# Expert mix shared by ScalarE, VectorE and GpSimd, with plain fp32 matmuls there and in the single-head attention

## The reference

```python
x = x + tanh(g_xattn[0]) * L0_xattn(_layernorm(x), ctx, ...)   # 16 heads of 8
x = x + tanh(g_ffn[0])   * L0_ffn(_layernorm(x), ...)          # 8 experts, 2 per token
x = x + tanh(g_xattn[1]) * L1_xattn(_layernorm(x), ctx, ...)   # 16 heads of 64
x = x + tanh(g_ffn[1])   * L1_ffn(_layernorm(x), ...)          # the expert mix
x = x + tanh(g_xattn[2]) * L2_xattn(_layernorm(x), ctx, ...)   # one head of 128
x = x + tanh(g_ffn[2])   * L2_ffn(_layernorm(x), ...)          # 8 experts, 1 per token
x = x + tanh(g_xattn[3]) * L3_xattn(_layernorm(x), ctx, ...)   # 16 heads of 8
x = x + tanh(g_ffn[3])   * L3_ffn(_layernorm(x), ...)          # ternary weights
```

```python
gate = softmax(x @ gate_w + gate_b)
weights = gate * (gate >= 0.1)
weights = weights / where(sum(weights) == 0, 1, sum(weights))
for e in range(8):
    out = out + weights[:, e:e+1] * (x @ expert_w[e] + expert_b[e])
```

## Time and profile before

| | |
|---|---|
| median of 3 runs | 997.49 us (996.33 to 1000.16) |
| the profiled execution's own time | 996.21 us |
| its span in the profile | 994.4 us, 1.8 us less |
| mean granted TensorE clock | 0.847 |
| PE busy over the span | 767.9 us (77%) |
| DVE | 519.3 us (52%) |
| ACT | 378.3 us (38%) |
| POOL | 278.8 us (28%) |

### The profile page before, as it was taken

One profiled execution on the slowest core, in us unless ns is written; L12 is line 12 of the kernel. 1 busy time (PEld: TensorE's weight loads), 2 busy tenths in 40 slices (PEclk: granted clock), 3 DMA queues, 4 the chain that ended last, 5 costly groups with the idle time before them and its releaser, 6 DMA issues.

```text
span 994.4 us, 18119 instructions
## 1 busy us (share of the span) xinstructions
PE 767.9 (77%) x6805; PEld 652.2 (66%) x6805; DVE 519.3 (52%) x1610; ACT 378.3 (38%) x886; POOL 278.8 (28%) x229
## 2 busy tenths in 40 slices
PE   4789872878959898989997556994486975988874
PEld 3567750777858787979786334774374964767764
DVE  5467461352234776666664878424242333778562
ACT  5455530333424654646461001210132554555450
POOL 4344316514332450212020000000305334344031
PEclk9999795798979999999998877555596986999996
DMA  7533625525733000000001000000432634321001
GB/s 182 131 89 104 195 74 172 136 73 162 208 102 102 19 23 1 2 1 2 1 1 64 0 1 0 1 1 28 147 97 85 181 105 118 104 64 34 1 12 32
DMA packets 60546, 70.95 MB, mean 71 GB/s; under 512 B 7036, under 2 KB 40717, under 8 KB 60461
## 3 DMA queue, kind: packets, MB, share of 16 engines
q1 hardware_dynamic: 57389, 63.48, 22.6%
q0 software_dynamic: 3072, 6.30, 2.1%
HBM read 48.86 MB, written 20.91 MB: 70 GB/s over the span
## 4 chain that ended last, share of the span: by engine, by line
PE 53%; DVE 19%; issue 8%; DMA 7%; ACT 6%; POOL 6%; SPq 0%; POOLq 0%; DVEq 0%; ACTq 0%
PE banks L1346 6%; PE banks L1362 5%; PE banks L1027 4%; PE banks L1438 4%; POOL xs L648 4%; DMA xs<-xn,slot 3%; PE banks L1028 3%; PE banks L1029 3%; DVE x L2221 3%; PE banks L1447 3%; PE banks L1069 3%; PE banks L1458 3%; PE banks L1155 3%; PE banks L1178 2%; PE banks L1167 2%
## 5 line engine op out<-in xcount | busy, mean ns | idle before, releaser
L898 ACT ACTIVATE hT<-banks,wup 128x128 f32<-128x128 f32 x304 | 85.6, 371 | 155.4 <-PE banks L1346 139.2
L1346 PE MATMUL banks<-xTs,wup 128*128 128x128 f32 x608 | 95.2, 309 | 21.2 <-issue 12.9
L1346 PEld LDWEIGHTS banks<-xTs,wup 128*128 128x128 f32 x608 | 88.1, 223 | 25.0 <-issue 24.9
L573 POOL TENSOR_TENSOR kbd<-k,const 96x1248 fp32r<-96x1248 f32 x32 | 72.3, 2266 | 70.4 <-PE banks L1155 68.2
L815 ACT ACTIVATE pT<-banks 77x512 f32<-77x512 f32 x128 | 69.0, 589 | 57.8 <-PE banks L1155 57.7
L1362 PE MATMUL banks<-wd,hT 128*128 x608 | 87.7, 292 | 3.8 <-ACT hT L898 3.8
L556 POOL TENSOR_TENSOR rstd<-vv,const 128x4 f32<-128x4 f32 x24 | 24.3, 1014 | 223.0 <-DVE vv L1662 223.0
L1362 PEld LDWEIGHTS banks<-wd,hT 128*128 128x128 f32 x608 | 81.1, 208 | 4.3 <-issue 4.2
L648 POOL DMA_INDIRECT xs<-xn,slot x48 | 46.5, 969 | 121.8 <-DVE slot L1960 89.8
L2072 DVE COPY ysb<-banks 128x128 f32<-128x128 f32 x76 | 22.0, 289 | 107.9 <-PE banks L1362 93.1
L611 POOL TENSOR_TENSOR sh<-sh,rd 128x616 f32<-128x616 f32 x32 | 38.9, 1216 | 129.4 <-DVE rd L1715 128.8
(11 more groups left out here) (323 smaller groups left out, 1787.3 us busy)
## 6 DMA issues: line engine op xcount, KB each, us to landing
wup<-in_up SPq DMA_DIRECT2D x76, 258.0 KB
q<-queries SPq DMA_DIRECT2D x24, 256.0 KB, 4.3
queries<-qc SPq DMA_DIRECT2D x8, 512.0 KB, 2.7
wd<-in_down SPq DMA_DIRECT2D x8, 512.0 KB, 5.1
ys<-ysb SPq DMA_DIRECT2D x16, 256.0 KB
k<-keys SPq DMA_DIRECT2D x24, 156.0 KB, 3.6
xs<-zt SPq DMA_DIRECT2D x2, 1472.0 KB, 11.5
keys<-kc SPq DMA_DIRECT2D x8, 312.0 KB, 3.4
```

Source lines behind the costliest of these rows:

```text
L573: pool.tensor_tensor(kbd[b % NB8][0:96, :, :, :].bitcast(F32R), kb, m, ALU.mult).then_inc(h8.kbd, 1)
L898: ins = act.activation(hT[T % 3][:, c, :], ps[:, T % 2, c * P:c * P + P], func, bias=wup[T % NW][:, HID + c:HID + c + 1])
L1346: ins = pe.matmul(ps[:, T % 2, c * P:c * P + P], w_[:, c * P:c * P + P], xTs[T % 3][:, :], start=True, stop=True)
```

## The change

In the mix, the products of experts 0 to 3 (i = 0) are made by ScalarE into buffers `mtmp`, those of experts 4 to 7 by VectorE onto `x` as before. GpSimd adds up ScalarE's products and the bias rows and adds the sum to `x` (`mixed_sum`). The units alternate between the two halves (`mixed_unit`). Units and gate logits are single fp32 matmuls on unrounded tokens `xT`, in two buffers; fronts in `PLAIN` (those of both stages) have no remainder. The gate of group g + 1 is computed during group g, that of group 0 and the first two units during the last group of `heads64`; eight small operations follow the exponential instead of eleven. ScalarE normalises the tokens of four fronts that VectorE did. In `head128`, q and both score products are single fp32 matmuls; k and v stay split. The front moves ahead of the second scores, and VectorE adds a group's output one group later. The split of `head128`'s weights moves ahead of the mix. GpSimd no longer splits the expert weights.

```diff
-        ON_ACT = (*range(0, NG), *range(6 * NG, 7 * NG + 1))
+        ON_ACT = (*range(0, NG), *range(3 * NG + 1, 4 * NG + 1), *range(6 * NG, 7 * NG + 1))
+        PLAIN = (*range(3 * NG, 5 * NG),)
...
+            def mixed_sum(g):
+                m = mtmp[g % 2]
+                pool.wait_ge(mx.act, 4 * (g + 1))
+                pool.tensor_tensor(m[:, :, 0:2, :], m[:, :, 0:2, :], m[:, :, 2:4, :], ALU.add).then_inc(su.plink, 1)
+                pool.wait_ge(su.plink, NG + 3 * g)
+                pool.tensor_tensor(m[:, :, 0, :], m[:, :, 0, :], m[:, :, 1, :], ALU.add).then_inc(su.plink, 1)
+                pool.wait_ge(su.plink, NG + 3 * g + 1)
+                pool.wait_ge(mx.xb, g + 1)
+                pool.tensor_tensor(m[:, :, 0, :], m[:, :, 0, :], m[:, :, 4, :], ALU.add).then_inc(su.plink, 1)
+                pool.wait_ge(su.plink, NG + 3 * g + 2)
+                pool.wait_ge(mx.half, 4 * (g + 1))
+                xt = x[:, GB * g:GB * g + GB, :]
+                pool.tensor_tensor(xt, xt, m[:, :, 0, :], ALU.add).then_inc(mx.x, 1)
...
             def mixed():
+                def products(g, t):
+                    if t == 0:
+                        act.wait_ge(mx.c, g + 1)
+                        if g >= 2:
+                            act.wait_ge(mx.x, g - 1)
+                    act.wait_ge(mx.o, 8 * g + 2 * t + 1)
+                    for e in range(4):
+                        ins = copy(mtmp[g % 2][:, t, e, :], ps[:, (8 * g + 2 * t) % 6, e * P:e * P + P],
+                                   scale=cw8[:, GB * (g % 2) + t, e:e + 1])
+                    ins.then_inc(mx.act, 1)
+                for g in range(NG):
+                    n = g + 3 * NG + 1
+                    scaled(next_group(g), n)
+                    products(g, 0)
+                    act.wait_ge(mx.ct_mm, g + 1)
+                    copy(cT[:, 0, :], ps[0:GB * E, 6, 0:P]).then_inc(mx.ct, 1)
+                    products(g, 1)
+                    front(n)
+                    products(g, 2)
+                    act.wait_ge(mx.b_mm, g + 1)
+                    copy(mtmp[g % 2][:, :, 4, :], ps[:, 6, :].rearrange("p (t d) -> p t d", t=GB)).then_inc(mx.xb, 1)
+                    if g < NG - 1:
+                        gate_exp(g + 1)
+                    products(g, 3)
...
+            def mixed_unit(g, v):
+                U, t, i = 8 * g + v, v // 2, v % 2
+                if U >= 6:
+                    pe.wait_ge((mx.act, mx.half)[i], (U - 6) // 2 + 1)
+                pe.matmul(ps[:, U % 6, :], xT[(g + 3 * NG) % 2][:, t * P:t * P + P], l1raw[:, 3, 512 * i:512 * i + 512],
+                          start=True, stop=True).then_inc(mx.o, 1)
             def mixed():
+                for g in range(NG):
+                    for v in range(2 * GB):
+                        if g or v >= 2:
+                            mixed_unit(g, v)
+                        if v == 1:
+                            pe.wait_ge(mx.c, g + 1)
+                            if g:
+                                pe.wait_ge(mx.xb, g)
+                            pe.transpose(ps[0:GB * E, 6, 0:P], ...
+                        if v == 3:
+                            if g:
+                                pe.wait_ge(mx.d, g + 1)
+                            front(g + 3 * NG + 1)
+                            pe.wait_ge(mx.ct, g + 1)
+                            pe.matmul(ps[:, 6, :], cT[:, 0, :], b2m[1]...).then_inc(mx.b_mm, 1)
+                        if v == 5 and g < NG - 1:
+                            mixed_logits(g + 1)
...
-                            ins = split3(ps[:, 3, b * SP:b * SP + SP], tokens([z[:, :] for z in q_], b),
-                                         tuple(z[:, b, :] for z in k_))
+                            ins = pe.matmul(ps[:, 3, b * SP:b * SP + SP], q2[i][:, b * P:b * P + P], k2[i][:, b, :],
+                                            start=True, stop=True)
-                        split3(ps[:, 0, :], tuple(w_[:, 0, :] for w_ in w2), xs).then_inc(h1.qmm, 1)
+                        pe.matmul(ps[:, 0, :], b_raw[:, 0:P], xT[g % 2], start=True, stop=True).then_inc(h1.qmm, 1)
...
+                def during():
+                    mixed_weights(0)
+                    front_a(1, 3 * NG + 1)
+                attend(h64, NG - 1, add, None, during)
...
             def mixed():
+                wait_done(dve, "h64", 1)
+                front_b(1, 3 * NG + 1)
+                dve.wait_ge(mx.c, 1)
+                for g in range(NG):
+                    n = g + 3 * NG + 2
+                    weighted(g, 0)
+                    front_a((g + 2) % NG, n)
+                    weighted(g, 2)
+                    if g < NG - 1:
+                        mixed_gate(g + 1)
+                        front_b((g + 2) % NG, n)
+                        mixed_weights(g + 1)
+                        dve.wait_ge(mx.c, g + 2)
```

More of the change, by code:

```diff
@@ L213, in build @@
         wregion = [top[0], wend]
+        mtmp = [place(f"mtmp{i}", [P, GB, 5, D], F32, wregion) for i in range(2)]
+        wregion = [top[0], wend]
         wf = place("wf", [P, HID], F32R, wregion)
@@ L307, in build, with split_upto @@
         back_in = (mo.gat0, mo.gat1)
-        ON_ACT = (*range(0, NG), *range(6 * NG, 7 * NG + 1))
+        ON_ACT = (*range(0, NG), *range(3 * NG + 1, 4 * NG + 1), *range(6 * NG, 7 * NG + 1))
+        PLAIN = (*range(3 * NG, 5 * NG),)
+        xT = (xT_even[:, :], xT_odd[:, :])
+        def split_upto(n):
+            return sum(m not in DROPPED and m not in PLAIN for m in range(n + 1))
         def shifts(n):
@@ L694, in _ @@
             ins.then_inc(su.scratch, 1)
-            for g in range(0, NG):
-                rsqrt_front(g + 4 * NG + 1)
+            for g in range(NG):
+                rsqrt_front(g + 3 * NG + 2)
+                mixed_sum(g)
+            for g in range(0, NG - 1):
+                rsqrt_front(g + 4 * NG + 2)
             spread(2)
@@ L1466, in heads64, with first_units, mixed_logits @@
                     front(g + 2 * NG + 2)
-                attend(h64, NG - 1, scores, own_values, values, project)
+                mixed_logits(0)
+                def first_units(between):
+                    pe.wait_ge(h64.sub, 4 * B)
+                    mixed_unit(0, 0)
+                    mixed_unit(0, 1)
+                    between()
+                attend(h64, NG - 1, scores, own_values, values, project, first_units)
+            def mixed_logits(g):
+                pe.wait_ge(fr.lo, upto(g + 3 * NG))
+                pe.wait_ge(ld.r, 16 * 9)
+                for t in range(GB):
+                    ins = pe.matmul(ps[:, 7, t * 16:t * 16 + E], xT[(g + 3 * NG) % 2][:, t * P:t * P + P], rraw[:, 0:E],
+                                    start=True, stop=True)
+                ins.then_inc(mx.r, 1)
@@ L1532, in head128 @@
                             o_ = ps[0:SK, 5, b * P:b * P + P]
-                            split3(o_, tuple(z[:, b, 0:SK] for z in k_), tokens([z[:, :] for z in q_], b), stop=False)
+                            pe.matmul(o_, k2[i][:, b, 0:SK], q2[i][:, b * P:b * P + P], start=True, stop=False)
                             ins = pe.matmul(o_, const[0:GB, C_SELB + b * SK:C_SELB + b * SK + SK], nT2[:, :],
@@ L2271, in head128 @@
[L2271 to L2283 removed]
+                        dve.tensor_copy(nT2[:, :], ps[0:GB, 3, 384:384 + P]).then_inc(h1.nT, 1)
```

256 lines of the change are left out of this document (109 added, 147 removed).

## The result

The changed kernel takes 965.54 us (median of 4 runs, 963.98 to 969.16) against 996.91 us (4 runs, 995.85 to 1000.16): ratio 0.9685, 95% interval 0.965 to 0.9721. The forecast was 964 us in a range of 944 to 986. The total was hit, but in part by luck: the mix gained 6.9 us less than forecast, the attention and the stages behind it 8.4 us more, and these misses nearly cancel.

What follows compares the result with a forecast made beforehand. It took the mix as bound by VectorE's serial products and gate, on which TensorE waits, and the attention by TensorE at half clock; 22.4 + 10 = 32.4 us off 996.21 gave 963.8, stated as 964, range 944 to 986.

Steps and rivals of the forecast that it cites:

- start of the mix: Last attention block before the mix: early weights, statistics, two units and logits make it 2.3 us longer.
- weights to end of unit 7, all groups, with last products: Mix: TensorE's stretch after the weights, 8.0 us a group at full clock; group 0 10.0, last products 2.1.
- end of unit 7 to the next weights, 3 x: Mix: landing, products, gate and small operations take 5.0 us between groups, with TensorE idle for 3.2.
- mix in sum: Whole expert mix: 59.4 us against 81.8, 22.4 us less.
- single-head attention: Stage after the mix: 10 us less, bounds 2 and 20.
- 20.2 us a group: Mix: upper bound of a group, six units at 1.71 and the rest doubled, plus 5.0; about 4.5 us less.
- so it hides behind the next group: Mix: GpSimd's sums, 7.5 us a group, are wanted only later and stay hidden, even at twice the cost.
- The rival about GpSimd: Mix: sums over 15 us a group hold back buffers two groups on, about 12 us lost, 976 us; chance 0.06.
- Which of the two depends on the clock at which the stage is entered: Attention: the clock at entry decides between half clock, gaining 2 us, and full clock, gaining 20.
- that is no gain: Attention at half clock: savings and losses of the fp32 products and new order cancel; only the first group gives 2 us.
- 9.7 us for a group at full clock: Attention: a group's period at full clock is 9.7 us, against 14.4 at half clock before.
- Half of 20: Attention: half of the 20 us full-clock gain was taken, 10 less.

Runs made afterwards that it cites:

- e1: Changed kernel without GpSimd's sums in the mix, one add of 8 columns a group instead: 957.0 us, ratio 0.9577.
- e2: Changed kernel with GpSimd's sums started only when the next weights are ready, the last after the next front's normalisation: 957.76 us, ratio 0.9614.
- e8: Changed kernel with GpSimd's first sum of each group cut into eight of 128x128: 965.58 us, ratio 0.9666.
- e3: Changed kernel with the next group's gate and weights placed ahead of VectorE's second pair of tiles: 954.3 us, ratio 0.9525.
- e6: Changed kernel with the gate ahead of VectorE's second pair of tiles and GpSimd's sums held back as well: 952.21 us, ratio 0.9535.
- e4: Changed kernel with four unread fp32 matmuls in each of TensorE's three waits for the weights: 968.49 us, ratio 0.9675.
- e5: Kernel before with only the single-head attention's part of the change (products, order, late addition): 984.53 us, ratio 0.9869.
- e7: Kernel before with only the attention's q and score products as single fp32 matmuls, order unchanged: 987.85 us, ratio 0.9912.

## Why the total was right and three of its terms were not

Ahead of the mix, code that the change does not touch ran 6.9 us longer in the first profiled execution than before and 1.2 in the second, so the spans differ by 27.0 and 32.9 us. The parts from the mix on, measured in the first, add up to 33.9 us less.

| term | predicted us | measured |
|---|---|---|
| start of the mix | +2.3 | +2.2 |
| weights to end of unit 7, all groups, with last products | 42.1 | 40.6 |
| end of unit 7 to the next weights, 3 x | 3 x 5.0 = 15.0 | 3 x 7.8 = 23.4 |
| mix in sum | -22.4 | -15.5 |
| single-head attention | -10 | -14.0 |
| stages behind | 0 | -4.4 |
| total, medians | -32.4 | -31.4 |

(42.1 is the prediction's 10.0 + 3 x 15.0 + 2.1 less the 15.0. Measured are 10.9, 9.6, 9.4 and 10.65. Mix in sum: 2.2 + 64.1 = 66.3 from the same point as in the earlier trace rows, 81.8 there.) Two of the prediction's sums do not come out as written: the parts of the way from unit 7 to the weights make 5.1 us, not 5.0, and 20.2 us a group would be 6.8 us less than before, not 4.5. The first would move the forecast by 0.4 us, the second moves only a bound.

**The failed step is GpSimd's "so it hides behind the next group".** The sums' length was right, and no one waited for their result. But they run beside the gate, and two operations of VectorE stand until they end. Removing the sums (e1), moving them (e2) and cutting them (e8) each take that wait away (2.9, 2.9 and 3.2 us are left of 5.9), so this is shown. The gate's 5.0 us were sound: without the collision it is 7.8 - 3.04 = 4.76, and TensorE's idle 2.9 against 3.2 predicted. The rival about GpSimd looked for the wrong victim: the buffers two groups on, at twice the price, where the victim was the next small operation of VectorE, at the normal price. The Trainium skill has the rule in "GPSIMD Engine Reference", Key points: GpSimd shares its SBUF interfaces with VectorE, and contention arises with VectorE instructions that have two SBUF inputs or run in a 2-port mode. The trace agrees (L2277 has two such inputs, 2.33 us for 0.16). The prediction did not weigh it. It could have: the trace of the kernel before shows such a collision, ahead of the first expert stage (timeline, before). An operation of VectorE on 128x8 elements with two inputs in SBUF lasts 2.23 us and ends 0.03 us behind GpSimd's; its neighbour of the same size takes 0.15.

```profile
98.33 2.27 POOL L573 TENSOR_TENSOR kbd<-k,const 96x1248 fp32r<-96x1248 f32 x1
98.40 2.23 DVE L2026 SCALAR_TENSOR_TENSOR mb<-mv,rstd 128x8 f32<-128x8 f32 x1 [0.79 <-POOL rstd L578]
...
100.55 0.15 DVE L2027 TENSOR_TENSOR rs<-mv,rstd 128x8 f32<-128x8 f32 x1
```

**The gate one group ahead.** That VectorE's order keeps the gate behind unit 7 was read rightly. What that order costs is read from four kernels: with the sums where the change has them 18.1 us of mix (64.0 against e3's 45.9), with the sums moved 9.8 (e2's 53.2 against e6's 43.4). The collision in turn costs 10.8 us of mix with this order (64.0 against 53.2) and 2.5 with the gate first (45.9 against 43.4).

**The clock in the mix.** It fell in each group, but behind idles of 5.9 us where 3.2 were forecast: windows of the changed kernel around the gate of group 1.

```profile
549.60:556.50 6.90, 4.20 (x14) 1.94 (x13) 3.92 (x17) 1.90 (x7) 0.56 (x1) 0.99 0.00 0
556.50:563.30 6.80, 3.58 (x5) 1.44 (x6) 3.45 (x4) 3.28 (x12) 5.57 (x4) 0.50 0.00 1
563.30:573.50 10.20, 7.91 (x27) 3.75 (x25) 7.53 (x37) 3.71 (x12) 1.17 (x2) 1.00 0.00 1
```

And two stretches of e2, behind its first and its third gate, each of 2.9 us idle:

```profile
548.80:552.30 3.50, 3.31 (x5) 1.43 (x6) 0.49 (x2) 3.18 (x12) 3.14 (x2) 0.51 0.01 2
577.15:579.15 2.00, 2.00 (x7) 1.00 (x8) 0.33 (x1) 2.00 (x9) 1.91 (x1) 1.00 0.00 0
```

The changed kernel's burst starts at 0.50 at 559.72 and is at full clock from 563.3. It cost 9.5 us a group for the predicted 8.0, where 2.0 of penalty were allowed. That each burst begins at the low clock after idle time is also the rule quoted in the prediction from the Trainium skill, "TensorE: Matmul & The Clock Gate"; the trace agrees for each of these idles of 5.9 us. For 2.9 us it agrees in two gates of e2 and not in the third, which stays at 1.00; e1 (2.9) and e8 (3.2) show the same. So near the idle that was forecast the clock falls in some gates only. It was never the large item: e4 bought back 4.9 us of it with the idle filled.

**The attention.** "Which of the two depends on the clock at which the stage is entered" is disproved by e5: entered at 0.50, it reaches 1.00 by itself. The changed kernel entered at full clock, 0.97 over its first group of 6.4 us, and had 0.66 over its last 21.9. The working at half clock ("that is no gain") was right for the form of the products; no run has a whole middle group of the new order at 0.50, so for the order it is untested. Windows of one group from q to q at 0.50, the kernel before, then e7:

```profile
635.97:650.40 14.43, 14.06 (x64) 11.67 (x65) 6.40 (x26) 2.90 (x5) 1.01 (x1) 0.50 0.00 0
635.07:649.32 14.25, 13.88 (x55) 9.99 (x55) 5.24 (x26) 2.90 (x5) 1.01 (x1) 0.50 0.00 0
```

That is 0.2 us for the form, and 1.2 in the first group (6.7 for 7.9), where 2 were predicted. The other 4.5 of e7's 5.8 us fall in the two stretches in which its clock rose. So what the prediction had wrong is what brings the clock back: the new form and order do it inside the stage. Why they do is not shown. Its 9.7 us for a group at full clock stand against 9.85 and 10.06 measured at 0.84 and 0.83. Half of 20 happened to lie near 14: that is luck.

**What stays open.** The stages behind the attention took 311 to 320 us with the same code, and their lengths stay the same when a kernel is run twice (314.2 both times). Kernels that differ only in the mix have 318.4 (e3), 319.5 (e8) and 314.0 (e2), those that differ only in the attention 314.3 and 313.1 against 318.6 before. The clock falls at other places in each; that this is the cause is argued, not shown. The attention took 48 to 54 us with one code. In e2 and e6 a part of that can be read: the last sum, held back behind the normalisation, meets the statistics that follow it. The timeline of e6 (in the changed kernel the same lines of the statistics take 0.17 us):

```profile
585.46 2.38 POOL L692 TENSOR_TENSOR mtmp<-mtmp 128x1024 f32<-128x1024 f32 x1 [2.84 <-DVE xn L1760]
...
585.82 2.04 DVE L1723 TENSOR_TENSOR fs<-st 128x4 f32<-128x4 f32 x1
...
588.04 1.18 DVE L1727 TENSOR_SCALAR mv<-fs 128x4 f32<-128x4 f32 x1
```

Two more follow behind the other sums, 4.9 us together, and TensorE waits up to 2.4 us for the maxima. In e2 the first two groups of the attention take 20.3 us where the changed kernel has 16.2: that is the 4.0 us by which its stage is longer. In the second of them the clock is lower too (0.67 against 0.84), and how the 4.0 divide is not shown. So moving the sums moved the collision at the end of the mix; it did not remove it there. e4 gained 4.9 us and e8 8.5 us in the mix, and neither gained in the total. That a shorter stage can pay less than it saves is seen; by what rule is not. Nor does a run separate the parts of the change in the mix (ScalarE's half of the products, the plain matmuls, the shorter gate): only the collision, the order of the gate and the clock were tried.

## What to carry to other kernels

When work moves to GpSimd, look not only for who waits for its result but for which of VectorE's operations on SBUF run at that moment: put GpSimd's large additions where VectorE reads PSUM, or cut them small (here that made the mix 8.5 us shorter and the total no shorter). Then look where the moved addition lands: in e2 it was the next stage's statistics. "One group ahead" is worth what the order of the slowest program lets through: here moving VectorE's second pair of products behind the gate was worth more, a ratio of 0.9525 for 0.9685 (e3). And a stage's gain is not the total's when the clock moves with it; judge by the ratio.

## What was not expected of the hardware

- One operation of VectorE on four elements a partition, with two inputs in SBUF, waits for the whole running GpSimd instruction: 2.33 us beside 2.34, 1.12 beside 1.26, 0.44 beside 0.45. A tensor_tensor of the first gate (L2274) took 1.04 us for 0.19 beside a sum of the attention (L622). The reciprocal (0.18, e3) and the products that read PSUM and SBUF (0.34) ran beside a sum at their usual length. A normalisation from SBUF to SBUF with one tensor input was held as well: 5.02 us for four, 1.1 when alone (e1).
- Half clock under full load lasts: 98% busy for 23.9 us at 0.50 (e7), while e5 left it after 8.8 us.
- A single fp32 matmul of 512 columns followed by another of its kind takes 0.90 us at full clock (four instructions in 1.80, e3); the three rounded ones took 0.69. What the plain form alone is worth in the mix no run shows.
